# Rounding the last group's row tiles on GpSimd, and summing the bias map with two products with ones

## What is computed

```python
xn = _layernorm(x, axis=-1)
x = x + _L0_gnn_ref(xn, W, edge_weight, src, dst) + _L0_mix_ref(xn[None], Wq, bq, Wk, bk, Wv, bv, weights)[0]
x = x + _L0_ffn_ref(_layernorm(x, axis=-1)[None], w_gate, w_up, w_down)[0]
```

```python
scale = 127.0 / jnp.clip(jnp.max(jnp.abs(x), axis=-1, keepdims=True), 1e-05)
xq = jnp.clip(jnp.round(x * scale), -128.0, 127.0) / scale
```

## Time and profile before

| what | us |
|---|---|
| median of 3 runs | 1640.52 (1638.73 to 1642.57) |
| profiled execution, its own time | 1638.98 |
| its span | 1637.2 |
| PE busy | 1618.5 (99%) |
| DVE busy | 1126.4 (69%) |
| ACT busy | 506.6 (31%) |
| POOL busy | 716.5 (44%) |

### The profile page before, as it was taken

One profiled execution on the slowest core, in us unless ns is written; L12 is line 12 of the kernel. 1 busy time (PEld: TensorE's weight loads), 2 busy tenths in 40 slices (PEclk: granted clock), 3 DMA queues, 4 the chain that ended last, 5 costly groups with the idle time before them and its releaser, 6 DMA issues.

```text
span 1637.2 us, 22023 instructions
## 1 busy us (share of the span) xinstructions
PE 1618.5 (99%) x7680; PEld 1331.2 (81%) x7680; DVE 1126.4 (69%) x2622; ACT 506.6 (31%) x649; POOL 716.5 (44%) x577
## 2 busy tenths in 40 slices
PE   7999999999999999999999999999999999999998
PEld 7899999877777887877877888888888888888665
DVE  7887793676777766755565567677758667576796
ACT  5744311321121111123310124333333324233464
POOL 2011556577777777777688705542130120300200
PEclk9999999999999999999999999999999999999999
DMA  9999888754776665557866655586393563742954
GB/s 325 370 407 351 290 284 265 217 130 111 181 202 168 164 153 142 129 150 185 224 141 145 130 172 166 176 197 187 94 211 105 126 161 99 159 129 71 243 163 126
DMA packets 164010, 304.94 MB, mean 186 GB/s; under 512 B 62856, under 2 KB 103624, under 8 KB 163945
## 3 DMA queue, kind: packets, MB, share of 16 engines
q1 hardware_dynamic: 77853, 204.77, 39.0%
q0 software_dynamic: 80272, 82.55, 24.4%
q10 hardware_dynamic: 5820, 16.88, 2.9%
HBM read 202.88 MB, written 101.24 MB: 186 GB/s over the span
## 4 chain that ended last, share of the span: by engine, by line
PE 93%; DVE 5%; issue 1%; ACT 1%; DMA 0%; ACTq 0%; DVEq 0%; SPq 0%
PE PS L403 25%; PE PS L405 25%; PE PS L404 25%; PE PS L1659 5%; PE PS L1661 5%; PE PS L1660 5%; PE PS L1726 2%; PE PS L1910 1%; PE PS L1676 1%; DVE fin L1594 1%; PE PS L1940 1%; DVE hid L1568 1%; DVE h_sc L1571 1%; DVE hid L1578 0%; DVE stats L1165 0%
## 5 line engine op out<-in xcount | busy, mean ns | idle before, releaser
L748 POOL DMA_INDIRECT A_dense<-wtot,cell x333 | 539.9, 1621 | 210.6 <-DMA A_dense<-wtot,cell 110.6
L403 PE MATMUL PS<-AL,SH 125*128 125x500 f32 x784 | 306.0, 390 | 0.0
L405 PE MATMUL PS<-AH,SH 125*128 125x500 f32 x784 | 304.8, 389 | 0.0
L404 PE MATMUL PS<-AH,SL 125*128 125x500 f32 x784 | 304.4, 388 | 0.0
L403 PE MATMUL PS<-WL,xtH 128*125 128x512 f32 x640 | 252.2, 394 | 0.7 <-DVE xtL L1318 0.7
L404 PE MATMUL PS<-WH,xtL 128*125 128x512 f32 x640 | 251.9, 394 | 0.0
L405 PE MATMUL PS<-WH,xtH 128*125 128x512 f32 x640 | 251.7, 393 | 0.0
L1042 ACT ACTIVATE SH<-S 125x1024 fp32r<-125x1024 f32 x98 | 104.0, 1061 | 333.6 <-PE PS L405 333.6
L1432 DVE TENSOR_TENSOR SL<-S,SH 125x1024 fp32r<-125x1024 f32 x98 | 119.5, 1220 | 121.0 <-ACT SH L1042 121.0
L405 PEld LDWEIGHTS PS<-AH,SH 125*128 125x128 f32 x784 | 147.5, 188 | 31.6
L404 PEld LDWEIGHTS PS<-AH,SL 125*128 125x128 f32 x784 | 146.9, 187 | 31.1
(11 more groups left out here) (204 smaller groups left out, 2658.8 us busy)
## 6 DMA issues: line engine op xcount, KB each, us to landing
A_dense<-zeros POOLq DMA_DIRECT2D x40, 1280.0 KB, 8.6
xt<-xnT SPq DMA_DIRECT2D x60, 500.0 KB, 5.9
Araw<-A_dense SPq DMA_DIRECT2D x100, 250.0 KB, 2.8
Aside<-A_dense SPq DMA_DIRECT2D x100, 250.0 KB, 3.0
keyrow<-key_rows SPq DMA_DIRECT2D x42, 512.0 KB, 4.3
ewrow<-weight_rows SPq DMA_DIRECT2D x42, 512.0 KB, 5.6
xnT<-XT ACTq DMA_DIRECT2D x20, 500.0 KB, 7.6
zx<-in_x SPq DMA_DIRECT2D x20, 448.0 KB
```

Of the source, the lines that this page charges most:

```text
L403: nc.tensor.matmul(o, lh, rl, start=start, stop=False)
L404: nc.tensor.matmul(o, ll, rh, start=False, stop=False)
L405: return nc.tensor.matmul(o, lh, rh, start=False, stop=stop)
L748: pool.indirect_dma_start(cells[m], bass.IndirectOffsetOnAxis(cell[:, col:col + 1], 0), wtot[:, col:col + 1], None, compute_op=ALU.add).th ...
```

## The change

Two parts, and a shift that goes with the first.

The two rounding operations of the last group's four row tiles move from VectorE (`round_r`) to GpSimd, behind its last DMA; GpSimd waits for the scale of each tile (`s_f6`), and ScalarE's `integers` waits for GpSimd. VectorE leaves `round_r` early for that group. The statistics of the last group are taken at t = 4 (d = 0), 5 (d = 1) and 6 (d = 2, 3).

For the bias map, VectorE multiplies `bdqk` with the biases in steps k = 3 and 4 of the fold, into `turned` and `bb`, and adds the two at k = 5. TensorE then multiplies a 128x128 matrix of ones (`earlier[:, 0, :]`) with the sum, in two products of 512 columns, in place of the sixteen of 128. `s_bprod` is another name for the semaphore `s_second`, which stands at 32 by then.

```diff
-STATS_AT = (4, 6)
+STATS_AT = (4, 5, 6)
...
+        for d in range(GT):
+            c, n = rc[0:ROWS, d % 2, :], (TILES - GT + d) * 4
+            pool.wait_ge(s_f6, n + 3)
+            nc.gpsimd.tensor_scalar(c, c, f_sc[0:ROWS, d:d + 1], 127.0, ALU.mult, ALU.min).then_inc(s_key, 1)
+            pool.wait_ge(s_key, 4 + d)
+            nc.gpsimd.tensor_scalar(c, c, -128.0, ROUND, ALU.max, ALU.add).then_inc(s_rq[d % 2], 1)
...
+            if k in (3, 4):
+                dve.wait_ge(s_bdq, 4)
+                nc.vector.tensor_tensor(by_block((turned, bb)[k - 3][:, :]), bdqk[k - 3][:, :, :],
+                                        bias[:, k - 3, :, 0:1].to_broadcast([P, KT, P]), ALU.mult).then_inc(s_bprod, 1)
+            if k == 5:
+                dve.wait_ge(s_bprod, 34)
+                nc.vector.tensor_tensor(turned[:, :], turned[:, :], bb[:, :], ALU.add).then_inc(s_bprod, 1)
...
             dve.wait_ge(s_f6, n + 3)
+            if isinstance(g, int) and g == GROUPS - 1:
+                dve.sem_inc(s_f6, 1)
+                return
...
-                half = STATS_AT.index(t)
-                row_stats(GROUPS - 1, (2 * half, 2 * half + 1))
-                if half:
+                part = STATS_AT.index(t)
+                row_stats(GROUPS - 1, ((0,), (1,), (2, 3))[part])
+                if part == 2:
...
         def map_of_bias():
-            for j in range(KT):
-                for m in range(2):
-                    last = nc.tensor.matmul(by_block(two_banks(3))[:, j, :], bias[:, m, j, 0:1].to_broadcast([P, P]),
-                                            bdqk[m][:, j, :], start=m == 0 and j % (KT // 2) == 0, stop=m == 1,
-                                            skip_group_check=True)
+            pe.wait_ge(s_bprod, 35)
+            for c in range(2):
+                last = nc.tensor.matmul(PS[:, 6 + c, :], earlier[:, 0, :], turned[:, c * 512:(c + 1) * 512], start=True, stop=True)
```

More of the change, by code:

```diff
@@ L391, in layer_kernel @@
     s_bdq = sem("s_bdq")
+    s_bprod = s_second
     s_w2h = sem("s_w2h")
@@ L1141, in _ @@
                 transposed_x(1, HALF - 1)
-            if t == STATS_AT[1]:
+            if t == STATS_AT[-1]:
                 deviation(GROUPS - 1)
@@ L1611, in _ @@
             if t in STATS_AT:
-                half = STATS_AT.index(t)
-                row_stats(GROUPS - 1, (2 * half, 2 * half + 1))
-                if half:
+                part = STATS_AT.index(t)
+                row_stats(GROUPS - 1, ((0,), (1,), (2, 3))[part])
+                if part == 2:
                     row_moments(GROUPS - 1)
-            if t == STATS_AT[1] + 1:
+            if t == STATS_AT[-1] + 1:
                 inverse_deviation(GROUPS - 1)
```

## The result

| | median, us | range of its runs |
|---|---|---|
| before | 1640.52 | 1638.73 to 1642.57 |
| after | 1658.28 | 1657.85 to 1659.62 |

The ratio of after to before is 1.0106, 95% interval 1.0092 to 1.0119. The change makes the kernel 17.8 us slower. The forecast of 1638.5 us, its range of 1636.3 to 1643 and its side are wrong. The first rival, GpSimd too slow, names the right place, with a chance of 0.19; by its formula the price measured gives 1654.9 us.

The account below looks back on a forecast made before the run. The prediction took TensorE to bound the kernel, at 5.85 us a row tile. Savings of 1.82 us (bias map) and 0.24 us (t = 15), -2.06 in all, took the median 1640.52 to 1638.5 us, range 1636.3 to 1643.

Parts of the forecast that it names:

- GpSimd too slow: Rival, chance 0.19: GpSimd operations over 1.75 us hold TensorE by 2(X - 1.75) at each of four tiles.
- X: Price of one GpSimd rounding operation of 125x1024, put at 1.3 us; nothing lost up to 1.75.
- part 5: Last group's rounding on GpSimd: ScalarE's wait in `integers` is covered by slack, so the move costs nothing.
- T: Time ScalarE can begin `integers`, 1566.5 + 2X, put at 1569.1; as late as 1570.0 without loss.
- the beat: TensorE's own work for one feed-forward row tile, 5.85 us between transposes of hidden rows.
- Part 1: Bias map on TensorE: two products of 512 columns replace sixteen, 3.57 us become 1.75, saving 1.82 us.
- The rival of products as cheap as float32r ones: Bias map: four wide records take 0.95 us, saving 2.62, in all 1637.7 us; chance 0.05.
- Part 2: VectorE's three added operations for the bias map fit its idle time; 3.4 us cover the wait, cost nothing.
- Part 3: Last group's statistics at t = 4, 5, 6 fit the same VectorE idle time: cost and gain 0.
- Part 4: VectorE without the last group's rounding, 5.56 us less work: only 0.24 us gained, at t = 15.
- VectorE is the bound: Rival, feed-forward part: VectorE's removed rounding counts in full, -1.82 - 5.56, giving 1633.1 us; chance 0.05.
- Held VectorE: Rival: small L1576 waits for a GpSimd operation, `hq` starts at T + 1.16; under 0.1 us a tile.

Follow-up runs that it names:

- e1: Kernel before with the bias-map part alone (VectorE's three operations, two wide products): 1638.88 us, ratio 0.9986.
- e5: Kernel before plus twelve GpSimd operations of several forms on a free buffer, which nobody waits for: 1644.34 us, ratio 1.0022.
- e12: Kernel before plus twelve unwaited GpSimd operations of other forms, run for their prices: a single execution 1642.34 us, beside 1639.94 for before.
- e6: Changed kernel plus 36 unread TensorE products of 256 columns ahead of the transposes of t = 9, 11, 13, 15: 1655.86 us, ratio 1.0085 to before.
- e3: Changed kernel with ScalarE's integers asked for a row tile later, behind t = 9, 11, 13, 15: 1640.25 us, ratio 0.9994 to before.
- e4: Changed kernel with product and minimum back on VectorE, GpSimd doing only maximum and addition: 1641.56 us, ratio 1.0001 to before.
- e7: Kernel before with only the last group's statistics moved to t = 4, 5, 6: 1642.04 us, ratio 1.0005.
- e8: Changed kernel with GpSimd's rounding as one operation, product and addition, clips left out: 1639.85 us, ratio 0.9996 to before.
- e9: e1 with the last group's rounding on VectorE as one operation, product and addition without clips: 1637.84 us, ratio 0.9980 to before.
- e11: e8 with all other roundings of activations also as one operation, product and addition without clips: 1637.40 us, ratio 0.9984 to before.

## Why the prediction was wrong

**The step that failed is the price X in part 5**, "I take 1.3" with bounds of 1.0 to 1.6 from the memset and the affine select. In the sum the move to GpSimd stood at nothing; by the ratios of after and e1 it cost 19.7 us. Measured: 3.71 for product and minimum, 3.64 to 4.17 for maximum and addition. The two rows lie on GpSimd's fast side, where e5 and e12 also find the copy and product-and-addition (1.0 us for 1000 columns); the operations of the change are on the other side. The iota with 1.95 us for 336 columns, taken as the far bound only, stands for 5.9 us and was the row of a slow operation that the trace did have. With bounds of 1.6 and 5.9 and a slack of 1.75 in between, a chance of 0.19 for the rival was too low: nothing in the trace tied these operations to the cheap rows. Both signs that the prediction named for this came: longer operations, and TensorE idle before t = 9, 11, 13 and 15.

The page that spoke against the move, the Trainium skill, "GPSIMD Engine Reference", section "Elementwise — side-by-side cycle accounting", was nearer but low too. Estimated from it, X was 1.5 us for one input; the trace has 3.71 us for 1024 columns, 4.3 cycles of 1.2 GHz per column against the 1.8 to 2.6 cited, and 1.2 cycles for product and addition. The measurement decides.

**The mechanism of that rival was right.** The slack of part 5 was T = 1570.0, with transposes due at 1571.91 in before. In after they were due at 1571.33, which allows T = 1571.33 - 1.86 = 1569.47; ScalarE began at 1573.63, 4.16 us late, and the transposes were 4.12 late. The limit X = 1.75 becomes (1569.47 - 1565.63 - 0.11) / 2 = 1.87, with the measured steps between the operations. The rival's formula, 4 x 2(X - 1.75), gives 16.5 us for the mean X of 3.81; e6, with the clock kept up, shows 15.7 to 16.1. With the gains of 2.1 taken off, the rival would have had 1654.9 us, 3.4 under the result. e3 and e4 move the same slack: with a tile more of it the loss vanishes, and with one operation 0.7 us a tile remain.

**The clock was missing.** Of the 19.7 us over the beat, 3.6 to 4.0 come from tiles that TensorE works off at a granted clock of 0.70 to 0.79 behind a gap. No rival had it; it would not have changed the side. Loss by the traces up to t = 16: 19.7 - 0.24, less 1.86 for the bias map, is 17.6, and the medians have 17.8. The two profiled spans differ by 18.9; before the row tiles in question single executions lie up to some us apart, so the spans are not taken apart further.

**Part 1**: 1.82 us predicted, 1.86 in the trace, 2.3 by e1. The four wide records take 1.88 us together, near the 1.79 of sixteen narrow ones at 0.112, so the argument from L1708, that the columns set the price, fits. The rival of products as cheap as float32r ones, 0.95 for the four, falls by the trace; e1's interval alone would hold its 2.62.

**Part 2**: the wait costs nothing; sum done at 289.2 us (said: 288.5, in a trace that runs 0.8 us earlier there), cover 3.5 us.

**Part 3**: nothing gained or lost, by e7.

**Part 4**: 0.24 us at t = 15, seen in e8 and e9 where that interval is 5.85. "VectorE is the bound", -5.56 us, falls with it: in e8 two operations a pair of tiles are gone from VectorE and the beat is the same 5.85.

**Held VectorE** is a real mechanism whose size I had wrong both ways. VectorE isn't held for a whole GpSimd operation, as I assumed: L1593, which was L1576 in before, took its usual 0.14 us at 1568.61 in the midst of one, so `hq` doesn't go to T + 1.16 by it. But other operations are held. VectorE in after, beside GpSimd's operations of 1569.43 to 1573.60 and of 1587.03 to 1590.67:

```profile
1568.79 0.84 DVE L1595 TENSOR_SCALAR hid<-hid,h_sc 125x512 f32<-125x512 f32 x1
1569.66 1.13 DVE L1597 TENSOR_SCALAR hid<-hid 125x512 f32<-125x512 f32 x1
...
1571.91 0.80 DVE L1486 TENSOR_SCALAR rc<-zr,group_mv,rstd 125x1024 f32<-125x1024 f32 x1
...
1589.92 1.29 DVE L1486 TENSOR_SCALAR rc<-zr,group_mv,rstd 125x1024 f32<-125x1024 f32 x1
```

L1595 takes 0.49 and L1597 0.43 us undisturbed, so they lose 0.35 and 0.70. L1486 at 1571.91, in the midst of a GpSimd operation, takes its usual 0.80. At 1589.92, 0.75 us before GpSimd's end, it takes 1.29 and ends 0.54 us behind it. For VectorE this is hidden in after under ScalarE's wait; it costs 3 us in e5, where VectorE has no room. GpSimd's side of it is not hidden: its second operation takes 4.17 and 4.16 us at t = 8 and 12, and 3.64 at t = 10 and 14, and ScalarE waits for its end. That makes some 1 us of the loss, an estimate from these four durations.

**Open.** The interval to t = 7 varies between profiles; among before, e1 and e9, which are the same there, it is 6.12, 7.03 and 6.91 us. VectorE waits there for rows of `zr` from DRAM, 0.8 us in e1, 0.9 in e8, 0.7 in e9 and 1.4 in e11, and not in before, e3, e6 and e7. It is the likely reason why ratios of e8 to e11 don't sort by the work they leave out, but I made no experiment on it.

## What to carry to other kernels

Work moved to an idle engine must be shorter there than the slack of whoever waits for it, and its price must come from a row of the same operations: when there is none, the bounds are the engine's cheapest and dearest rows, and a slack that lies between them covers nothing. Before moving a two-step operation, rewrite it: here product and addition alone took 1.1 us where product, minimum, maximum and addition took 7.6. A gap of 3 to 4 us in TensorE can cost more than itself: behind three of the four here the next tile ran at a lower clock.

## What the runs showed of the hardware

**GpSimd's price depends on which operations are asked for.** On 125 rows of float32, us: product and addition 1.03 to 1.15 and copy 1.02 for 1000 columns; one operation, product or maximum, 2.7; product and minimum, maximum and addition, product and subtraction, 3.6 to 3.7, and 1.93 for 500 columns.

**The two engines hold each other up near the start and near the end of GpSimd's operation, and not between.** The operations of VectorE that took longer beside GpSimd's lost at most 0.7 to 0.9 us, and they are of two kinds. Some began within some 0.5 us of GpSimd's start, and lost about the same beside an operation of 1.03 us (e5, 0.14 to 0.96) as beside one of 4.17 us (after, 0.43 to 1.13). The others were 512 or 1024 columns wide and began in its last 0.9 us; they ended 0.28 and 0.54 us behind it. In e4 it is always these: the rounding of `hid`, 0.43 us by itself, began at 1571.30 beside GpSimd's 1568.41 to 1572.16, and took 1.14 us. Between the two, as L1486 at 1571.91 in after, none took longer. GpSimd is held too: its own 3.64 became 4.17 in after, and in e12 a product and addition of 500 columns took 1.24 us in place of 0.68 beside a VectorE operation of 1024. The Trainium skill, "SBUF — State Buffer", section "Practical consequences", says that operations of VectorE and GpSimd that share a pair of ports exclude each other for the whole instruction; the trace agrees near both ends, and the rows between speak against it for the whole.

**TensorE's clock behind a gap**: after 4.4 us with 0.50 us of work the granted clock was 0.54 over the next 5.6 us, and the tile of 5.85 us took 8.32; with the gap filled by products it was 1.00, and the tile 5.86. Behind the waits of 0.5 to 0.6 us in e4 it stayed at 1.00.
